# A chunk's total factor read from the last row of the growing factors and spread by two DMAs, in a gated linear attention with routed experts on one core

## The reference, cut to what matters

```
gk = log_sigmoid(x @ Wgk1 @ Wgk2 + bgk2) / 16.0
# for each token t, per head:
state = state * exp(gk_t)[..., None] + v_t[..., None] * k_t[..., None, :]
out_t = einsum('bhvk,bhk->bhv', state, q_t)
```

## Time and profile before

| | us |
|---|---|
| median of 3 runs | 902.65 (901.77 to 903.55) |
| time of the profiled execution | 902.91 |
| its span on the core | 901.1 |
| mean granted clock of TensorE | 0.966 of full speed |

### The profile page before, as it was taken

How to read it: one execution, slowest core, us unless ns; L and a number is a source line. 1 busy time by engine, 2 the same in 40 slices (tenths; PEclk the granted TensorE clock), 3 DMA queues, 4 the chain that set the end, 5 groups by cost and what they waited for, 6 DMA issues and landing times.

```text
span 901.1 us, 24612 instructions
## 1 busy us (share of the span) xinstructions
PE 829.5 (92%) x6743; PEld 732.8 (81%) x6744; DVE 586.9 (65%) x1446; ACT 473.8 (53%) x1425; POOL 447.6 (50%) x452
## 2 busy tenths in 40 slices
PE   5599999999999999971899999999999999999994
PEld 4477777777777777850899999999999999999994
DVE  1578888888888888856256474564564654745743
ACT  1477777777777777730434434434445344344351
POOL 3357777777777777741134334333343343343332
PEclk9699999999999999975899999999999999999997
DMA  6931111111111111112922222222222222222221
GB/s 225 379 112 55 61 60 60 60 60 60 60 60 60 60 60 60 54 50 90 309 38 44 42 36 42 42 36 45 39 42 42 36 42 42 36 42 42 41 40 21
DMA packets 51449, 62.64 MB, mean 70 GB/s; under 512 B 6274, under 2 KB 46932, under 8 KB 51284
## 3 DMA queue, kind: packets, MB, share of 16 engines
q1 hardware_dynamic: 38548, 44.36, 15.2%
q0 software_dynamic: 12864, 17.83, 11.4%
HBM read 38.91 MB, written 23.27 MB: 69 GB/s over the span
## 4 chain that ended last, share of the span: by engine, by line
PE 75%; DVE 10%; issue 5%; ACT 4%; DVEq 2%; DMA 1%; SPq 1%; POOL 0%; ACTq 0%; POOLq 0%
PE p_s L1106 42%; PE p_gz L1106 10%; PE p_qk L1106 8%; PE p_o L1106 8%; DVE w_hi L876 4%; PE p_qk L1125 2%; PE p_tr L1106 2%; PE p_tr L1288 2%; ACT h2T L687 1%; ACT hT L687 1%; PE p_o L1125 1%; DVE host_o L889 1%; DMA w_all<-in_L_wmod_dram 1%; PE p_tr L1125 1%; DVE host_s_r L1090 1%
## 5 line engine op out<-in xcount | busy, mean ns | idle before, releaser
L668 POOL DMA_INDIRECT out_dram<-x,tok x68 | 166.9, 2455 | 311.9 <-DVE x L1083 296.2
L687 ACT ACTIVATE h2T<-p_tr,mods 128x128 f32<-128x128 f32 x136 | 55.0, 455 | 258.7 <-PE p_tr L1288 258.7
L1106 PE MATMUL p_s<-w_all_r,host_s_r 128*128 x544 | 143.2, 405 | 2.9 <-DVE host_s_r L1090 2.9
L1106 PEld LDWEIGHTS p_s<-w_all_r,host_s_r 128*128 128x128 f32 x544 | 98.2, 190 | 20.9 <-issue 3.3
L648 POOL DMA_INDIRECT expert_rows<-rows,pos x64 | 65.8, 1028 | 47.9 <-issue 32.4
L1079 DVE TENSOR_TENSOR ga<-p_s,b_all 128x256 f32<-128x256 f32 x68 | 28.8, 423 | 84.1 <-PE p_s L1106 83.9
L876 DVE TENSOR_TENSOR w_hi<-p_s,upto 128x1024 f32<-128x1024 f32 x64 | 77.8, 1216 | 0.2 <-PE p_s L1106 0.2
L1106 PE MATMUL p_s<-h2T,host_x 128*128 128x128 f32 x544 | 67.1, 276 | 3.8 <-DVE qkT_both L1042 2.8
L1106 PE MATMUL p_qk<-h2T,host_x 128*128 128x128 f32 x544 | 68.1, 279 | 2.5 <-ACT h2T L687 1.1
L1106 PEld LDWEIGHTS p_qk<-h2T,host_x 128*128 128x128 f32 x544 | 65.3, 196 | 3.4 <-issue 3.4
L1106 PEld LDWEIGHTS p_s<-h2T,host_x 128*128 128x128 f32 x544 | 63.6, 192 | 5.2 <-issue 4.5
(11 more groups left out here) (209 smaller groups left out, 1961.2 us busy)
## 6 DMA issues: line engine op xcount, KB each, us to landing
ln_host<-expert_rows SPq DMA_DIRECT2D x68, 136.0 KB, 2.1
host_x<-in_L_attn_x_dram SPq DMA_DIRECT2D x64, 128.0 KB, 2.1
w<-in_L_ffn_W_dram SPq DMA_DIRECT2D x8, 1024.0 KB, 11.7
w_all<-in_L_ffn_W_dram SPq DMA_DIRECT2D x8, 1024.0 KB, 12.3
out_dram<-x SPq DMA_DIRECT2D x32, 128.0 KB, 1.7
w_all<-in_L_wmod_dram SPq DMA_DIRECT2D x1, 1536.0 KB, 6.8
expert_rows<-pad_rows SPq DMA_DIRECT2D x8, 136.0 KB, 1.7
out_dram<-x,tok POOLq DMA_INDIRECT x68, 4.7
```

The costliest lines, as they stand in the source:

```text
L668: nc.gpsimd.indirect_dma_start(out=out, out_offset=bass.IndirectOffsetOnAxis(ap=tok[u][:, 0:1], axis=0), in_=y_out[u][:], in_offset=None, ...
L687: last = A.activation(dst[:, j, :], src[:, j * P:(j + 1) * P], ACT.Identity, scale=mods[:, which + 2 + j:which + 3 + j], bias=mods[:, whic ...
L1106: return nc.tensor.matmul(dst, lhsT, rhs, start=start, stop=stop, skip_group_check=True)
```

## The change

The total's matmul and ScalarE's `e_tot` go. The last row of `upto_half`'s running sums is the total minus half of the total, so the last row of `e_pos` holds the values that `e_tot` had. SP now stores that row (1 KB) into a DRAM tensor of one row, waits until it has landed, and loads it into `e_tot` on all 128 partitions. Its waits stand behind the store of the finished chunk, in every step with a front part, and in step 0 ahead of the experts' loads. GpSimd's `decay` waits for the loaded row, VectorE's `vn` for `e_neg` alone, and the scores on TensorE wait for `e_pos`, since they overwrite the bank from which it is made.

```diff
+    tot_row = nc.dram_tensor("chunk_factor", (1, D), F32, kind="Internal").ap()
...
                 if finish:
                     sp.wait_ge(x1_ready, s)
                     load(out[bass.ds((s - 1) * P, P), :], x1[v][:], x1_stored[v])
+                if front:
+
+                    f = s + 1
+                    sp.wait_ge(e_ready, f + 1)
+                    after(sp, decay_ready, f)
+                    load(tot_row, e_pos[v][P - 1:P, :], etot_stored)
+                    sp.wait_ge(etot_stored, 16 * (f + 1) if isinstance(f, int) else (f + 1) * 16)
+                    load(e_tot[:], tot_row.to_broadcast([P, D]), etot_loaded)
                 if isinstance(s, int) and s == 0:
...
-                    pool.wait_ge(e_ready, f + 1)
+                    wait_apart(pool, (etot_loaded, 16 * (f + 1) if isinstance(f, int) else (f + 1) * 16))
                     nc.gpsimd.tensor_tensor(
                         decay[v][:].rearrange("p (j h d) -> p j h d", j=KD, d=HD),
...
-                    A.activation(e_neg[:], p_cum[:, 0:D], ACT.Exp, scale=-q)
-                    after(act_e, decay_ready, f)
-                    A.activation(e_tot[:], p_cum[:, D:2 * D], ACT.Exp, scale=q / 2)
+                    A.activation(e_neg[:], p_cum[:, 0:D], ACT.Exp, scale=-q).then_inc(e_neg_ready, 1)
                     after(act_e, o_ln_ready, f - 1)
+                    after(act_e, decay_ready, f - 1)
                     A.activation(e_pos[v][:], p_cum[:, 0:D], ACT.Exp, scale=q).then_inc(e_ready, 1)
...
-                    dve.wait_ge(e_ready, f + 1)
+                    dve.wait_ge(e_neg_ready, f + 1)
...
                         pe.wait_ge(vn_ready, 1)
+                    pe.wait_ge(e_ready, s + 1)
                     after(pe, u_taken, s)
...
-                    for n, sums in enumerate((upto_half, ones)):
-                        last = mm(p_cum[:, n * D:(n + 1) * D], sums[:], gz_s[:, D:2 * D], True, True)
-                    last.then_inc(cum_ready, 1)
+                    mm(p_cum[:, 0:D], upto_half[:], gz_s[:, D:2 * D], True, True).then_inc(cum_ready, 1)
```

More of the change, by code:

```diff
@@ L322, in build @@
         e_ready = sem("e_ready")
+        e_neg_ready = sem("e_neg_ready")
+        etot_stored = sem("etot_stored")
+        etot_loaded = sem("etot_loaded")
         decay_ready = sem("decay_ready")
```

## The result

The changed kernel takes 955.53 us (median of 4 runs, 953.41 to 958.19) against 902.93 (901.77 to 903.55) for the kernel before: a ratio of 1.0584 [1.0566, 1.0602], 52.6 us more. The profiled execution, the slowest of the four, took 958.19 us, with a span of 956.4 us and a mean granted clock of 0.945.

The account below looks back on a forecast made before the run. VectorE's loop (projection, residual, statistics, `vn`, `rows`, transposes, scores, masks) was taken to set the steady pace. 902.91 + 26.9 - 1.6 + 1.5 - 1.7 + 1.5 = 929.5 us, range 917 to 945.

Parts of the forecast that it names:

- SP in the first steps: Step 0: SP's wait delays the expert loads to 50.85 us, chunk 3 lands at 82.7 instead of 52.3: +26.9 us.
- The rival that had chunk 3 land by its own issue: First steps: expert loads do not hold chunk 3 up; issued at 70.0, landed at 72.1 us, total 919; chance 0.07.
- The two corrections, -1.6 and +1.5: After the start's stall: TensorE work done during it gives back 1.6 us; a lower clock in gate projections costs 1.5.
- The matmul by ones at 0: Steady steps: removing it from TensorE gains 0, since VectorE's `rows` is late next; 13.3 us at full price.
- ScalarE's e_tot, -1.7: Steady steps: without this exponential `vn` starts 0.06 us earlier a step, 29 steps: -1.7 us.
- The pair's lag, 4.2 us: Steady steps: store and load in series put `decay` 4.2 us after the end of `e_pos`; ends 3.4 and 6 us.
- the value taken is +1.5: Steady steps: `decay` comes 2.2 us later, just covered at 4.2 us lag; cost 0 to +25, taken as +1.5 us.
- The second rival: Steady steps: at 6 us lag the two DMAs set the pace, `rows` 1.8 us late every second step: 953; chance 0.14.

Follow-up runs that it names:

- the kernel without matmul and exponential: Changed kernel, but chunks 0 and 1 keep the matmul by ones and ScalarE's exponential; the DMAs begin with chunk 2: 930.52 us.
- the lag alone: Kernel before, keeping matmul and exponential, plus the DMA pair from chunk 2 into a tile nobody reads, with `decay` waiting for it: 928.46 us.
- the other order: GpSimd sends the routed rows before `decay` and the state: 931.53 us on the changed kernel, 905.01 us on the kernel before.
- the faster order of GpSimd: Kernel before, but GpSimd makes `decay`, then sends the routed rows, then makes the state: 898.95 us.

## Why the prediction was wrong

The sum had +26.8 us for the start and -0.2 for the steady steps. The runs gave 25.0 and 27.7.

*SP in the first steps: right, in mechanism and nearly in size.* Chunk 3's statistics came 31.97 us behind the first expert load, forecast 31.95 (82.8 - 50.85). They came 2 us earlier than forecast because that load went out at 48.77 instead of 50.85: the store ahead of it was issued at 47.26, where the forecast had 48.6, and the next issue came 1.1 us behind it, where 1.7 to its landing had been taken from a store of 128 KB. (The terms of the 50.85 add up to 50.8, and the landing of 8.0 us should be 8.1; neither changes anything.) The rival that had chunk 3 land by its own issue fell: issued at 69.17, it kept VectorE waiting until 80.74.

*The two corrections, -1.6 and +1.5: right in their sum, by luck.* The prediction had them cancel to -0.1. Together they came to +0.2 (the scores of step 2 are 25.0 us late, the statistics 24.8), but neither happened as told. The outputs of step 1 were not done in the stall: TensorE waited for VectorE with them until 81.85. So from the statistics to the scores it took 5.9 us, not 4.1. And the low clock fell into that stretch (0.55 from 84 to 86 us): the gate projection at 87.70 took 0.73 us, not 1.22.

*The matmul by ones at 0: right to about 1 us in the kernel before.* VectorE's loop sets the pace, and without the matmul TensorE waits for `rows` (0.35 us at 230.52). Beside the lag, the kernel without matmul and exponential was 2.1 us slower, not faster.

*ScalarE's e_tot, -1.7: too much.* The sum took a gain of 0.06 us in each of 29 steps. VectorE's idle time ahead of `vn` (L956 before, L968 after, in the groups above) was 1.1 us in all steps together and fell to 0.6: a gain of 0.5 at most.

*The pair's lag, 4.2 us: nearly right, in part by luck.* It was 4.48 in the step shown. The store took 1.1 us where 1.7 was forecast, the load 3.1 where 2.1 was, and the two errors went against each other.

*The step that failed: "So the delay is just covered, by GpSimd's idle time and this buffer", with "the value taken is +1.5".* Measured: 25.8 us for the lag alone, 27.7 with the matmul gone. The cover was tested for who waits on a semaphore behind GpSimd, and there it held: 0.9 us at the buffer. It was not tested for what GpSimd's shifted instructions then run beside. The prediction's list of what is queued behind `decay` ended with "the next normalisation"; that one was the price. In the kernel before, it starts 2.07 us ahead of `wt_a` (203.75 and 205.82), and `qbd` behind it is nearly through when `wt_a` starts. In the changed kernel it starts 0.51 us ahead (226.86 and 227.37), so that the pair lies on top of `wt_a`, and VectorE, which sets the pace, is held for 1.5 us in 13 of the steps.

The Trainium skill (SBUF — State Buffer, section "SBUF: two separate sides") has the rule that would have spoken against this step: VectorE and GpSimd share a pair of ports under an exclusive lock, and a VectorE instruction with two inputs in SBUF (against a GpSimd instruction that reads SBUF), or one in a fast mode, waits until the GpSimd instruction that holds it is through. The runs agree for `wt_a`: it ends as `qbd` ends (229.12 and 229.09), an input from PSUM frees it, the type alone does not. They go further in one point: `wt_a` is held past the normalisation's end, through `qbd` as well. In one point they differ: by that rule the one that starts first has the ports, but `wt_a` passed in 0.32 us where it started 0.26 us behind the normalisation's recorded start (81.18 and 80.92 in the run of the lag alone). There the measurement decides. Whether L966 and L968, with one input in SBUF, were held for a fast mode no trace shows.

The second rival's 953 us came near the measured time, but for another reason. Its lag, 6 us, was not there, and the wait that it priced was not either.

Left open: why the one-hot's own instruction, with two inputs in SBUF, takes its usual 0.16 us beside GpSimd's normalisation (at 239.48, within 238.63 to 239.85). How much of the 6 us in the five longest intervals is the clock and how much what made it fall was not parted. Whether the indirect DMA or `decay` holds the output norm in the other order was read from timelines, not tested. Issuing the expert loads ahead of the first pair, with the DMAs kept for chunks 0 and 1, was not tried, nor the faster order of GpSimd in the changed kernel.

## What to carry to other kernels

When a wait moves an engine by some microseconds, don't stop at the semaphores behind it: lay its shifted instructions over those of the engine that sets the pace, and look for GpSimd instructions that come to run beside a VectorE instruction on SBUF operands. A wait put into a queue that issues loads in program order delays every load behind it; the once-only steps at the start can cost as much as all steady steps. And a removed matmul is worth what the stage's loop gives, however full TensorE looks.

## What the runs showed of the hardware

- A VectorE instruction of 0.22 us (`wt_a`) took 1.75 to 1.81 us where it started 0.45 to 0.51 us behind the first of two GpSimd instructions in a row (but for two cases of 0.21 and 0.22), and 0.22 to 0.32 where it started 0.01 to 0.26 us behind. One of 0.48 us (the output norm's second) took 1.01 where it started 0.38 us behind GpSimd's instruction for an indirect DMA.
- Spreading 1 KB to 128 partitions by one DMA took 6.3 us from a row in SBUF and 3.1 us from a row in DRAM, so that store and load together (4.5 us from `e_pos` to `decay`) beat the single transfer (6.5). While the single one ran, the DMA engines moved 28 GB/s at a busy share of 0.83 (196 to 198 us of its trace).
